# Four graph hops: eight chained column steps per batch become one scan in PSUM

## The reference, cut to what matters

```
src2 = concatenate([src, dst]);  dst2 = concatenate([dst, src]);  e2 = concatenate([e, e])
e2 = e2 / segment_sum(e2, dst2)[dst2]                     # 4 heads of 32 numbers; self edges count 0
f(y) = segment_sum(y[src2] * e2, dst2)                    # one "hop"
k1 = f(x);  k2 = f(x + k1/3);  k3 = f(x + (k2 - k1/3));  k4 = f(x + (k1 - k2 + k3))
y = x + 0.125 * (k1 + 3*(k2 + k3) + k4)
```

## Time and profile before

| | us |
|---|---|
| median of the runs of the kernel before (3 runs, 4771.27 to 4777.51) | 4773.82 |
| the profiled execution, its own time | 4777.98 |
| its span, first to last instruction | 4776.1 |
| DVE busy in the span | 2278.5 |
| POOL busy in the span | 2985.9 |
| ACT busy in the span | 1021.3 |

### The profile page before, as it was taken

One profiled execution on the slowest core, in us unless ns is written; L12 is line 12 of the kernel. 1 busy time (PEld: TensorE's weight loads), 2 busy tenths in 40 slices (PEclk: granted clock), 3 DMA queues, 4 the chain that ended last, 5 costly groups with the idle time before them and its releaser, 6 DMA issues.

```text
span 4776.1 us, 26543 instructions
## 1 busy us (share of the span) xinstructions
PE 915.8 (19%) x5636; PEld 782.7 (16%) x5636; DVE 2278.5 (48%) x7031; ACT 1021.3 (21%) x2440; POOL 2985.9 (63%) x2952
## 2 busy tenths in 40 slices
PE   0656676751000286000000000000000000000000
PEld 0655565651000264000000000000000000000000
DVE  2976544441000399545444556545645455533233
ACT  0212666610000287000000111001100011113233
POOL 2687777767777300766656666566665666656675
PEclk6877878885555699555555555555555555555555
DMA  8343333332111276333334555545554344445454
GB/s 255 74 61 63 65 58 60 60 53 49 23 23 23 76 258 221 90 89 97 92 104 153 192 182 193 168 145 193 201 169 162 121 134 148 133 115 157 120 160 130
DMA packets 311301, 581.70 MB, mean 122 GB/s; under 512 B 93184, under 2 KB 171574, under 8 KB 311138
## 3 DMA queue, kind: packets, MB, share of 16 engines
q1 hardware_dynamic: 189682, 383.10, 23.9%
q0 software_dynamic: 116576, 169.55, 16.7%
q10 hardware_dynamic: 4880, 27.34, 1.9%
HBM read 332.00 MB, written 247.75 MB: 121 GB/s over the span
## 4 chain that ended last, share of the span: by engine, by line
DVE 33%; another core or an unknown queue 19%; issue 14%; POOL 6%; DMA 2%; ACT 1%; PE 0%; SPq 0%; DVEq 0%; POOLq 0%; ACTq 0%
DVE psum L1178 9%; DVE z_even L1178 8%; DVE us L1162 4%; POOL gx L1101 3%; POOL ag L1287 3%; DVE tn L1152 3%; DVE psum L1156 2%; DVE stats L790 2%; DVE z_even L1156 1%; DVE xa L926 1%; DMA ag<-agg 1%; ACT normed L820 1%; DVE res L939 1%; DVE mv L794 1%
## 5 line engine op out<-in xcount | busy, mean ns | idle before, releaser
L1101 POOL DMA_INDIRECT gx<-u,far_row x1176 | 1109.7, 944 | 540.6 <-issue 347.0
L1101 POOL DMA_INDIRECT gx<-x,far_i x392 | 371.6, 948 | 466.6 <-DMA x<-normed 290.7
L1132 ACT ACTIVATE psum<-us 128x512 f32<-128x512 f32 x288 | 173.1, 601 | 1573.3 <-DVE us L1162 863.2
L1178 DVE SCALAR_TENSOR_TENSOR psum<-z_even,cont,psum 128x128 f32<-128x128 f32 x784 | 278.3, 355 | 444.0 <-remote 202.8
L1287 POOL DMA_INDIRECT ag<-total,fin_idx x390 | 378.0, 969 | 173.3 <-issue 115.3
L865 POOL DMA_INDIRECT edge_s<-edge_d,edge_id x392 | 396.3, 1011 | 134.2 <-issue 127.4
L1178 DVE SCALAR_TENSOR_TENSOR z_even<-psum,cont,z_even 128x128 f32<-128x128 f32 x780 | 271.5, 348 | 427.0 <-remote 191.5
L1122 PE MATMUL psum<-last_z,chain 128*128 128x128 f32 x8 | 3.2, 501 | 2298.7 <-DVE last_z L1230 2298.7
L321 POOL DMA_INDIRECT agg<-summed,sc_idx x196 | 330.7, 1687 | 134.2 <-issue 125.4
L1122 PEld LDWEIGHTS psum<-last_z,chain 128*128 128x128 f32 x8 | 2.0, 310 | 2299.7 <-DVE last_z L1230 2299.7
L820 ACT ACTIVATE normed<-res,shift,rstd 128x128 f32<-128x128 f32 (+1 forms) x782 | 313.9, 480 | 29.3 <-remote 14.5
(11 more groups left out here) (172 smaller groups left out, 3391.9 us busy)
## 6 DMA issues: line engine op xcount, KB each, us to landing
u<-us SPq DMA_DIRECT2D x144, 512.0 KB
total<-tn SPq DMA_DIRECT2D x144, 512.0 KB
tp<-total SPq DMA_DIRECT2D x98, 512.0 KB
agg<-zero ACTq DMA_DIRECT2D x7, 3811.5 KB
ag<-agg SPq DMA_DIRECT2D x65, 396.0 KB
x<-normed SPq DMA_DIRECT2D x65, 387.0 KB
xc<-x SPq DMA_DIRECT2D x65, 387.0 KB
tp<-u SPq DMA_DIRECT2D x49, 512.0 KB
```

Of the source, the lines that this page charges most:

```text
L1101: g.indirect_dma_start(gx[b % 4][:, j * width:(j + 1) * width], None, source[:, :], bass.IndirectOffsetOnAxis(ap=idx[:, c:c + 1], axis=0)) ...
L1178: v.scalar_tensor_tensor(column(b, j), prev, cont[:, c:c + 1], column(b, j), ALU.mult, ALU.add).then_inc(run_set, 1)
```

## The change

All columns of a batch now lie in PSUM together, turned so that a number's eight columns are side by side (`z_all`, 128x1024, two banks; element (f, j) at f*8 + j). One instruction weighs the whole batch into that order, so it writes PSUM with a stride of 8 elements. `go_on` adds the kept last column of the batch before to column 0 (one 128x128 instruction with stride 8). One `tensor_tensor_scan` of 128x1024 then makes all running sums: its factor is 0 at the first column of each number and `cont` elsewhere. `keep_last` copies the last column to `last_z`. One instruction divides. The factors must stand in a tensor of the same 128x1024 shape: ACT copies them out for each batch into one of two buffers `goes_on` (`spread`), two batches' factors ahead, from `cont_in`, which is `cont` with zeros at the first column of each piece. `inv` lies in SBUF as a whole. There are now 50 pieces per hop, 48 batches and two halves.

```diff
-        inv_even = psum[:, 1024 + C * H:1024 + C * H + C * H // 2].rearrange("p (c h) -> p c h", h=H)
-        inv_odd = sb("inv_odd", [128, C // 2, H])
-        carry = bank[1][:, 0:D]
+        inv = sb("inv", [128, C, H])
+        carry = bank[6][:, 0:D]
+        cont_in = sb("cont_in", [128, C])
...
-            v.tensor_copy(inv_even, by_parity[:, :, :, 0])
-            v.tensor_copy(inv_odd[:, :, :], by_parity[:, :, :, 1])
+            v.tensor_copy(inv[:, :, :], e_sum[:, :, :].rearrange("p h c -> p c h"))
+            v.tensor_copy(cont_in[:, :], cont[:, :]).then_inc(cont_set, 1)
+            v.wait_ge(cont_set, 1)
+            v.memset(cont_in[:, :].rearrange("p (b j) -> p b j", j=B)[:, :, 0], 0.0).then_inc(cont_set, 1)
+            v.memset(cont_in[:, C - B // 2:C - B // 2 + 1], 0.0).then_inc(cont_set, 1)
...
-        z_even = [sb(f"z_even{i}", [128, B // 2, D], F32, held) for i in range(2)]
-        z_odd = [bank[i].rearrange("p (j f) -> p j f", f=D) for i in range(2)]
+        z_all = psum[:, 0:B * D]
+        goes_on = [sb(f"goes_on{i}", [128, B * D], F32, held) for i in range(2)]
+        PIECES = [(b, 0, B) for b in range(NB - 1)] + [(NB - 1, 0, B // 2), (NB - 1, B // 2, B)]
...
             def hop_scalar(act):
+                def spread(i):
+                    b, c0, c1 = PIECES[i]
+                    if i >= 2:
+                        act.wait_ge(run_set, summed_up(i - 2, h))
...
+                    act.copy(goes_on[i % 2][:, 0:n * D].rearrange("p (f j) -> p f j", j=n),
+                             cont_in[:, b * B + c0:b * B + c1].unsqueeze(1).to_broadcast([128, D, n])
+                             ).then_inc(on_set, 1)
+                spread(0)
+                for b in range(NB):
+                    spread(b + 1)
...
-                def run_on(b, j):
-                    if c >= 2:
-                        v.wait_ge(run_set, run0 + c - 1)
-                    prev = column(b, j - 1) if j else column(b - 1, B - 1)
-                    v.scalar_tensor_tensor(column(b, j), prev, cont[:, c:c + 1], column(b, j), ALU.mult, ALU.add
-                                           ).then_inc(run_set, 1)
+                def weigh(i):
+                    b, c0, c1, z, zf = piece(i)
+                    if h or i:
+                        v.wait_ge(last_kept, h * NPC + i)
...
+                            v.wait_ge(us_set, done + b)
+                    return v.tensor_tensor(zf.rearrange("p (h f) j -> p j h f", h=H),
+                                           by_head(gxv(b % 4)[:, c0:c1, 0:D]),
+                                           per_head(wt[:, b * B + c0:b * B + c1, :]), ALU.mult)
+                def go_on(i):
...
+                    v.scalar_tensor_tensor(zf[:, :, 0], last_z[:, :], cont[:, c:c + 1], zf[:, :, 0],
+                                           ALU.mult, ALU.add).then_inc(run_set, 1)
+                def add_up_runs(i):
...
+                    v.wait_ge(on_set, h * NPC + i + 1)
+                    v.tensor_tensor_scan(z, goes_on[i % 2][:, 0:(c1 - c0) * D], z, 0.0, ALU.mult, ALU.add
+                                         ).then_inc(run_set, 1)
+                def keep_last(i):
...
+                    v.tensor_copy(last_z[:, :], zf[:, :, c1 - c0 - 1]).then_inc(last_kept, 1)
+                def divide(i):
+                    return v.tensor_tensor(by_head(us[b % 3][:, c0:c1, :]), zf.rearrange("p (h f) j -> p j h f", h=H),
+                                           per_head(inv[:, b * B + c0:b * B + c1, :]), ALU.mult)
                 for b in range(NB - 1):
                     v.wait_ge(g_in[b % 4], landed(b))
-                    for i in range(2):
-                        weigh(b, 0, B, i).then_inc(z_set, 1)
+                    weigh(b).then_inc(z_set, 1)
                     if h and b >= 1:
                         add_total(b - 1, 0)
...
-                    for j in range(B):
-                        run_on(b, j)
-                        if h and b >= 1 and j == 3:
-                            add_total(b - 1, 1)
+                    go_on(b)
+                    if h and b >= 1:
+                        add_total(b - 1, 1)
+                    add_up_runs(b)
+                    keep_last(b)
...
-                    for i in range(2):
-                        divide(b, 0, B, i).then_inc(us_set, 1)
+                    divide(b).then_inc(us_set, 1)
```

More of the change, by code:

```diff
@@ L1093, in hop_gpsimd @@
                     if b >= 4:
-                        g.wait_ge(z_set, (done + b - 3) * 2)
+                        g.wait_ge(z_set, done + b - 3)
                         if h == 0:
@@ L1132, in hop_scalar @@
                             act.mul(shared, half(us[b % 3][:, :, :], i), share).then_inc(shared_set, 1)
-                else:
-                    for b in range(NB):
+                    elif h == 0:
                         act.wait_ge(g_in[b % 4], landed(b))
@@ L1208, in hop_vector @@
                     room_for_total(b)
-                v.wait_ge(z_part, (h + 1) * 2)
-                for j in range(m):
-                    run_on(b, j)
-                v.wait_ge(run_set, run0 + b * B + m - 1)
+                v.wait_ge(z_part, h + 1)
+                go_on(i)
+                add_up_runs(i)
+                keep_last(i)
                 if h < 3:
@@ L1223, in hop_vector @@
                 v.wait_ge(g_in[b % 4], landed(b))
-                for i in range(2):
-                    weigh(b, m, B, i).then_inc(z_set, 1)
-                v.wait_ge(z_set, (done + b + 1) * 2)
-                for j in range(m, B):
-                    run_on(b, j)
-                v.wait_ge(run_set, run0 + C - 1)
-                v.tensor_copy(last_z[:, :], column(b, B - 1)).then_inc(last_kept, 1)
-                for i in range(2):
-                    divide(b, m, B, i).then_inc(us_set, 1)
+                weigh(i + 1).then_inc(z_set, 1)
+                v.wait_ge(z_set, done + b + 1)
+                go_on(i + 1)
+                add_up_runs(i + 1)
+                keep_last(i + 1)
+                divide(i + 1).then_inc(us_set, 1)
                 if h:
-                    v.wait_ge(us_set, (done + b + 1) * 2)
+                    v.wait_ge(us_set, done + b + 1)
                     v.scalar_tensor_tensor(tn[b % 3][:, m:B, :], us[b % 3][:, m:B, :], share, tp[b % 3][:, m:B, :],
```

73 lines of the change are left out of this document (39 added, 34 removed).

## The result

The changed kernel takes 4665.96 us (median of 4 runs, 4662.01 to 4667.12) beside 4773.07 us for the kernel before (4 runs): a ratio of 0.977, 95% interval 0.975 to 0.979. It is faster by 107 us where 294 had been forecast, outside the range. The profiled execution took 4666.2 us, 111.8 less than that of before.

A forecast was written before the change was run, and what follows sets the result against it. No engine full; in the hops POOL's gathers set 10.0 us per batch, plus pauses for a late DVE. Pauses 227.5 and ends 67 give 294.5; 4778.0 - 294.5 = 4483.5, forecast 4480 us, range 4445 to 4635.

The forecast's parts named there:

- That cadence is POOL's floor: 8 x 1.25 = 10.0 us per batch: In the hops, gathers start 1.25 us apart, so POOL needs at least 10.0 us per batch, 490 us per hop.
- the 227.5 us for pauses: POOL's 48 pauses ahead of gathers, 241.9 us, would go, except 0.30 us each: 227.5 us gained.
- At 1.40 us each that is 9.8 and 7.0 us, both below POOL's 10.0: DVE's new 7 instructions per batch (5 in hop 0) would keep up with POOL's pace even at 1.40 us each.
- the slow mode: In stretches of the hops a DVE instruction counts as finished only every 1.40 us; it ends when POOL stops.
- Durations: DVE's new instructions, each forecast from rows of the trace, would take 7.0 us per batch, 5.4 in hop 0.
- rivals B: Strided PSUM reads also cost a factor 1.8: batch 10.8 us, about 115 us gained, 4660 us; chance 6%.
- C: Strided PSUM access dearer still, DVE bounds every batch; at a factor of 2.5 a batch takes 14.0 us, 5190 us; 4%.
- the 0.4 us stall ahead of the second `tn`: In hops 1 to 3, `go_on` covers only 0.39 of ACT's 0.60 us scaling between the `tn`s: 0.4 us stall per batch.
- The ends: POOL's waits at the four hops' ends would fall from 103.0 us to 36, 9 each: 67 us gained.
- `keep_last` beside a gather: If each of 200 `keep_last` copies held up a gather 0.29 us, 58 us lost; an outer bound, not summed.
- Rival A: DVE's slow toll falls on each dependent step, not the count: batch about 11.2 us, 165 us gained, 4609 us; 20%.
- The last line: Forecast fails if the slow mode's 1.40 us is a delay, not a rate, or if ACT shares that count.

The follow-up runs named there:

- `pauses`: Changed kernel in which POOL, ahead of every fourth batch from the fifth on, waits until all batches issued so far are weighed; 4681.92 us.
- `four_more`: Changed kernel with four more DVE instructions behind each batch's divide, each clearing a column nobody reads; 4779.38 us.
- `before_half_2`: Kernel before with every second gather of hops 1 to 3 left out, on a chip with the limit; 4109.61 us.
- `before_paced`: Kernel before with a useless POOL instruction writing 208 numbers per partition behind each gather of the hops; 4793.28 us beside 4802.97 for the kernel before.
- `after_half`: Changed kernel with every second gather of hops 1 to 3 left out, on the chip without the limit; 3623.1 us.
- `bare`: Changed kernel without `go_on`, scan, ACT's factor copies and `keep_last` (but the one at a hop's end); 4663.61 us.
- `no_keep`: Changed kernel without `keep_last`, except in the last piece of a hop; 4653.92 us.
- `factors_once`: Changed kernel in which ACT writes the scan's factors only for the first two pieces of hop 0; 4659.4 us.
- `half_rows`: Changed kernel whose gathers in hops 1 to 3 fetch 64 rows instead of 128; 4695.1 us.
- `before_paced_less`: Kernel before with a useless POOL instruction writing 112 numbers per partition behind each gather of the hops; 4746.76 us beside 4802.97 for the kernel before.
- `pool_eight`: Changed kernel with a short POOL instruction behind every gather, eight per batch, on the chip without the limit; 4072.45 us beside 4068.43 for the kernel before.

## Why the prediction was wrong

*The step that failed* is "That cadence is POOL's floor: 8 x 1.25 = 10.0 us per batch". 1.25 us is what a gather takes when nothing holds it; POOL may issue only one per 1.40 us on average, beyond a credit at the start that I estimate at 20 gathers (in hop 0, 188 gathers pass at 1.25 us before the first slow one: 188 x (1 - 1.25/1.40)). The floor of a hop is 392 x 1.40 = 549 us less what is left of that credit. The hops of before took 577.8 us on average, so about 29 us of each were to be had, not 74 (294.5/4). From a hop's first gather to its last 2128.6 us passed in the four hops instead of 4 x 391 x 1.25 = 1955; the 174 us between are the whole miss in the hops: 294.5 - 174 = 121, and they became 122.5 us shorter. By the terms of the sum: the 227.5 us for pauses were mis-sized, since the way from first to last gather became only 54.0 us shorter (2182.6 to 2128.6); the rest of the hops, their ends, gave 68.5 us where 67 was forecast.

*Why I did not see it:* the pauses that POOL made for DVE were counted as pure loss. They were what kept POOL under its limit. `pauses` shows that such waits are free.

*"At 1.40 us each that is 9.8 and 7.0 us, both below POOL's 10.0":* the count was right (`four_more`: 12.6 and 15.4 us), and DVE did stop being late. That the slow mode was DVE's own affair was wrong: it is there only while POOL runs against its limit (`before_half_2`, `before_paced`). The prediction's own "It ends when POOL stops" pointed there, and was not followed up.

*Durations:* weigh 1.22 forecast, 1.229 measured; scan 2.23 and 2.287; keep 0.29 and 0.291; the copies on ACT at most 1.15, 1.032. The 7.0 us for a batch on DVE is what `after_half` shows to the tenth. These rows are from the four hops of the changed kernel:

```profile
L1211 DVE TENSOR_TENSOR_SCAN psum<-goes_on,psum 128x1024 f32<-128x1024 f32 x192 | 439.2, 2287 | 1.8
L1192 DVE TENSOR_TENSOR psum<-gx,psum 128x1024 f32<-128x1024 f32 x192 | 236.0, 1229 | 880.8 <-DMA gx<-u,far_row 620.7 <-DMA gx<-x,far_i 238.9 <-issue 21.1
L1217 DVE COPY last_z<-psum 128x128 f32<-128x128 f32 x200 | 58.3, 291 | 6.9
```

The stride of 8 in PSUM costs nothing, so rivals B and C are out, and the 0.4 us stall ahead of the second `tn` is there (58.9 us before 288 of them, half of which have it). DVE waits for gathers for 620.7 + 238.9 = 859.6 us.

*The ends:* 36 us for the four, 34.2 measured. *`keep_last` beside a gather:* I left its 58 us out of the sum, and that was right: in the row of L1106 shown behind `bare`, of 2020 to 2120 us, ten of the copies lie beside gathers and no gather is longer than 0.952 us. This agrees with the rule of the Trainium skill (VectorE: DVE Perf Modes, section Mode 2×_2P) that the two-port mode needs its operands in SBUF. `no_keep`, with hops 1.5 us shorter, could not show it, since at POOL's limit the time of a gather that is held up would be given back as that of a pause is.

*Rival A* (a batch of 11.2 us, 4609) gave the batch time, but by luck: DVE has no toll, since its steps follow each other at once at 2708.37 and 2708.57, and the batch is as long in `bare`, where most of the chain is gone. *The last line* of the forecast named ACT as what might share the count; `factors_once` excludes it. POOL itself was not named.

*Outside the hops* I took nothing to change. The hops began 4.9 us earlier, and the last stage, with POOL's gathers in it too, takes 578.9 us instead of 563.3: 122.5 + 4.9 - 15.6 = 111.8. On chips with the limit it takes 578 to 583 us in every run of the changed kernel that keeps all its gathers and adds nothing to DVE or POOL (`bare` and `pauses` 578, `half_rows` 583), 562 in `four_more`, where POOL is under its limit when the hops end, and 502 on the chip without the limit. That hop 3 passes on a used-up credit fits, but was not tested by itself.

*It could have been read before.* The gathers of the sort, ahead of the hops, show it in the trace of the kernel before, where POOL has nobody to wait for. The first 200 start 1.25 us apart, but for a few; from then on it is 1.40 us on average, by steps of 1.25, 1.40 and 2.10. Two windows, of a few gathers and of 44:

```profile
1371.22 1.10 POOL L865 DMA_INDIRECT edge_s<-edge_d,edge_id  x1 [0.30 <-issue]
1372.62 1.09 POOL L865 DMA_INDIRECT edge_s<-edge_d,edge_id  x1 [0.30 <-issue]
1374.02 0.94 POOL L865 DMA_INDIRECT edge_s<-edge_d,edge_id  x1 [0.30 <-issue]
1375.27 0.94 POOL L865 DMA_INDIRECT edge_s<-edge_d,edge_id  x1 [0.30 <-issue]
```
```profile
1362.82:1424.41 61.59, 5.33 (x24) 4.45 (x23) 4.53 (x21) 3.75 (x13) 47.63 (x44) 0.56 0.12 22
```

Of the three steps two are 1.40 us and one 1.25, and 44 gathers in 61.6 us are 1.40 us each, with DVE busy for 4.5 us of them. A group whose mean lies above its shortest, with no wait to explain it, asks for such a look.

*What stays open:* what the limit is made of; why a short instruction of POOL counts only for a while; and why it is POOL that is held up in `before_paced_less` where it is DVE in the kernel before. A kernel whose gathers fetch two columns each, which would halve their number, was not tried.

## What to carry to other kernels

Before you count an engine's pauses as gain, divide the time of the whole stretch by the number of its instructions and compare with every pace it shows elsewhere in the trace: here 577.8/392 = 1.47 us per gather lay just above a limit of 1.40. An engine's shortest cadence is no floor until a stretch as long as the one you forecast has run at it: here 200 gathers in a row had, and 392 could not. And when a slow mode has no cause in the trace, look for it in who else is running: slow that one down and see, as `before_paced` did.

## What the runs showed of the hardware

Gathers of POOL (indirect DMAs of 128 or 64 rows) are limited to one per 1.40 us on average, after a credit of some 20, on all chips of this study but one; idle time of POOL is credited (`pauses`). While POOL runs at 1.25 us, 14 instructions per batch on DVE come to finish one per 1.40 us on average; steps of 1.40, 2.10 and 2.80 us, multiples of 0.70, are common there, and 1.40 and 2.10 in the gathers of the sort. On the chip without the limit the kernel before takes 4068.43 us, 15% less. The trace itself differs in one thing that I found: it holds 15 semaphore updates per us there (`pool_eight`, 1760 to 1860 us), and 1.4 in a stretch of the changed kernel at the limit (2200 to 2300 us), that is one per 0.70 us, with as many DMA packets per gather; it is 1.4 already at 2020 to 2120 us, where the gathers still start 1.25 us apart. Where POOL stays under one gather per 1.40 us it holds 12.7 (`before_half_2`, 2900 to 3000 us).

A possible cause is that the path on which such records leave the core backs up and, once it is full, holds the engines. The Trainium skill's page NOTIFIC — the notification-queue block, section 7.1, says that the block's internal pipeline always holds its producers back rather than lose a record, and that its stall counter would show an engine throttled by it. No run here shows that rule at work: none read the counter or changed what is recorded, so this stays a guess. The executions of the changed kernel that only took the time were as long (4662.01 to 4667.12 us) as the profiled one (4666.2), which speaks against a cause that exists only while a profile is taken.
